# Attention and gated mixing on one Trainium2 core: another hand-written order of the second part's stages

## The chip, the cores and the metric

The kernel runs on one core of a Trainium2 chip. The metric is the device time of one execution in microseconds (us). The kernel before takes 1852.48 us (median of 3 runs, 1850.31 to 1857.23).

## What is computed

For 8 batches of 2048 tokens with 256 features: layer norm, Nystrom attention with 16 heads and 64 landmarks, an output product, layer norm, residual; then layer norm, a gated mixing block with a shift by one token, layer norm, residual. Cut to what matters:

```
k, q, v = heads(norm(x) @ Wk), heads(norm(x) @ Wq) / 4, heads(norm(x) @ Wv)
q_l, k_l = means of q and k over groups of 32 tokens         # 64 landmarks
s1 = softmax(q @ k_l.T)      s2 = softmax(q_l @ k_l.T)      s3 = softmax(q_l @ k.T)
z = pinv(s2)                                                # 6 iterations
x = x + norm((s1 @ (z @ (s3 @ v))) @ Wo + bo)
h = norm(x);  d = shift(h) - h
r = sigmoid(xr @ W_r.T),  k = relu(xk @ W_k.T) ** 2          # xr, xk: h mixed with shift(h) by mu_r, mu_k
x = x + norm(r * (k @ W_v.T))
```

## The kernel before

Part one computes the landmarks and the inverses of all batches. It is the same in both kernels and ends at about 415 us. Part two goes through the batches; each batch is cut into four tiles (0 to 3) of 512 tokens. A stage is a short piece of work on a tile, and its name stands for what every engine does for it:

- XA normalizes the input (VectorE, `xhat`), R transposes it (TensorE) and splits it into a high and a low half (ScalarE and VectorE, `xT`). AQ, AK and AV are the projections to queries, keys and values. KC copies the keys by 12 DMAs into `k_stack`.
- B1 and B2 multiply keys with the landmarks' queries, and VectorE takes row maxima (L1257). C1 and C2 multiply queries with the landmarks' keys, and VectorE takes token maxima (L1265). M spreads the row maxima into `q_stack`, which stage S loads by 24 DMAs.
- FS (0 to 7) scores keys against landmarks, ScalarE takes the exponential (L915), FV multiplies it with the values and VectorE adds to `uT`. W and V apply the inverse.
- D, E1 and E2 are the token scores of a tile: D transposes the maxima, E1 and E2 multiply, ScalarE takes the exponential (L938). H applies them. O is the output product; VectorE then adds the bias and takes the statistics of a norm.
- OA applies this norm (VectorE), and GpSimd adds the residual (`xm`, L737). N takes statistics of the sum, NA applies them (`x2h`), T transposes (ScalarE copies to `x2T`, GpSimd subtracts, `xkT`, L747), TA mixes (VectorE, `xrT` and `xkT`, L1338).
- GR is the gate's product (L1777, ScalarE L971 and GB), GK the keys' (L1787), G2 the last (L1799, VectorE multiplies with the gate into `ob`). GS takes statistics, GA applies them, and GpSimd adds the residual (L753). GO writes the tile; XR loads the residual.

TensorE writes to three pairs of PSUM tensors, `bank`, `wide` and `acc`, shared by all stages: B, C, FS and E use `wide`. A stage may write to a pair when the reader of its last use has drained it.

The order of part two is written out by hand. `PRO` lists (stage, tile) for the start; `BODY` lists (stage, tile, offset of the batch) for one turn and is run seven times; `LAST` is the last turn. `part2_program` walks the joined list on each engine and issues that engine's share of each stage, so all five engines work in the same order, and waits are on semaphores that count uses:

```
        order = [(name, c, 0) for name, c in PRO]
        order += [(name, c, b + d) for b in range(B - 1) for name, c, d in BODY if b + d >= 0]
        order += [(name, c, B - 1 + d) for name, c, d in LAST]
```

A stage with offset -1 belongs to the batch before: the second half of a batch (its gates above all) runs between the projections of the next. Such a stage is written below as GR(1) for tile 1.

Of the kernel before, what the change touches and what calls it, by code (L numbers as in the profile page):

```python
# [15 lines left out]
def sandwich(nc, x, Wk, Wq, Wv, Wo, bo, W_r, W_k, W_v, mu_r, mu_k, out):  # L16
# [10 lines left out]
    H, HS, M, ITERS = 16, 16, 64, 6  # L27
# [12 lines left out]
    with ctx:  # L40
# [55 lines left out]
        GR = 4  # L96
# [19 lines left out]
        X = [sb(f"X{s}", [P, PAIRS, M], c=part1) for s in ROWS]  # L116
# [199 lines left out]
        class Norm:  # L316
# [40 lines left out]
            def apply(self, dve, dst, src, g, c):  # L357
# [58 lines left out]
        PRO = [("R", 0), ("X", 2), ("X", 3), ("Q", 0), ("AK", 0), ("XA", 2),  # L416
# [3 lines left out]
        BODY = [("C1", 2, 0), ("R", 3, 0), ("GK", 1, -1), ("C2", 2, 0), ("O", 3, -1), ("B2", 2, 0), ("T", 2, -1),  # L420
# [53 lines left out]
        counted, used = (0, 0, 0), {}  # L474
# [1357 lines left out]
```

## Time and profile before

| | |
|---|---|
| median of 3 runs | 1852.48 us (1850.31 to 1857.23) |
| the profiled execution's own time | 1859.59 us |
| its span, first to last instruction | 1857.9 us |
| granted TensorE clock, mean | 0.945 |
| busy: TensorE / VectorE / ScalarE / GpSimd | 1575.4 / 1370.3 / 1041.2 / 278.4 us |
| first FS of the first batch | 492.17 us |
| from then, per batch | 164.6, then five times 170.8 |
| the last batch's first FS | 1685.59 us |

The trace gives the start of each instruction in us from the span's start, its duration, and in brackets how long its engine had sat idle before it and what released it. Instructions of a kind in a row are merged; x4 is their count, and the duration is that of all together.

### The profile page before, as it was taken

What the parts mean: (1) busy time and instruction counts of PE and PEld (TensorE: products, weight loads), DVE (VectorE), ACT (ScalarE), POOL (GpSimd) and SP (SyncE); (2) the same over time, 40 slices, a digit from 0 to 9 for tenths busy, and PEclk for the clock granted to TensorE, in tenths of its full rate; (3) what the DMA queues carried; (4) which work ended last, traced back from release to release, by engine and by line L of the source; (5) the groups of instructions that cost most, each with busy time, mean ns of one, the idle gap of its engine ahead of it and who ended that gap; (6) DMA issues with size and microseconds to landing.
All of it is one profiled execution on the core that took longest, in us unless ns stands there. A gap on an engine that the chain in (4) does not pass through costs nothing. (4 is left out here: it accounts for less than half of the span.)

```text
span 1857.9 us, 50685 instructions
## 1 busy us (share of the span) xinstructions
PE 1575.4 (85%) x21132; PEld 1087.1 (59%) x21132; DVE 1370.3 (74%) x3068; ACT 1041.2 (56%) x1663; POOL 278.4 (15%) x163
## 2 busy tenths in 40 slices
PE   4778888787689889899889998998989899988885
PEld 2768767773455564465456555644655565546453
DVE  6887777777558966895797579668947975795475
ACT  1689769972354465455545554654455455535452
POOL 5200020000001111121111111111211121110122
PEclk9789989998899999999999999999999999999898
DMA  8300100002211312131322122221213211221111
GB/s 272 97 5 4 60 22 29 3 26 67 72 41 42 73 54 56 50 80 34 92 54 58 50 58 69 58 55 50 73 41 92 54 51 55 61 58 33 36 35 35
DMA packets 125844, 104.66 MB, mean 56 GB/s; under 512 B 30513, under 2 KB 123569, under 8 KB 125617
## 3 DMA queue, kind: packets, MB, share of 16 engines
q1 hardware_dynamic: 125616, 101.42, 19.5%
q8 instruction: 169, 2.77, 0.6%
q14 instruction: 59, 0.48, 0.1%
HBM read 56.23 MB, written 19.92 MB: 41 GB/s over the span
## 5 line engine op out<-in xcount | busy, mean ns | idle before, releaser
L938 ACT ACTIVATE p<-wide 128x1024 f32<-128x1024 f32 x128 | 124.0, 1021 | 123.0 <-PE wide L1717 122.3
L1265 DVE TENSOR_REDUCE m<-wide 128x16 f16<-128x1024 f32 x128 | 150.6, 1218 | 39.9 <-PE wide L1601 39.6
L1777 PE MATMUL bank<-wrT,xrT 128*128 128x256 f32 x512 | 139.5, 433 | 43.8 <-ACT vv L904 35.9
L915 ACT ACTIVATE e<-wide 128x1024 f32<-128x1024 f32 x128 | 124.5, 1021 | 79.6 <-PE wide L1634 68.3
L1257 DVE TENSOR_REDUCE m<-wide 128x2 f32<-128x1024 f32 x128 | 150.0, 1215 | 2.9 <-PE wide L1581 2.9
L1777 PEld LDWEIGHTS bank<-wrT,xrT 128*128 128x128 f32 x512 | 109.4, 219 | 68.9 <-issue 39.8
L753 POOL TENSOR_TENSOR ob<-ob,xm 128x1024 f32<-128x1024 f32 x32 | 77.0, 2406 | 480.6 <-DVE ob L361 480.6
L1757 PE MATMUL bank<-wo,oT 128*128 128x256 f32 x512 | 120.9, 390 | 6.2 <-DVE xT L1225 3.6
L747 POOL TENSOR_TENSOR xkT<-x2T 128x1024 f32<-128x1024 f32 x32 | 60.7, 1897 | 430.5 <-ACT x2T L963 430.5
L1787 PE MATMUL acc<-xkT,wkT 128*128 128x512 f32 x256 | 118.8, 608 | 7.1 <-DVE xkT L1338 7.1
L737 POOL TENSOR_TENSOR xm<-yy,xres 128x1024 f32<-128x1024 f32 x32 | 78.2, 2443 | 307.0 <-DVE yy L361 163.9
L1799 PE MATMUL bank<-wvT,ka 128*128 128x256 f32 x512 | 119.3, 387 | 0.8 <-ACT x2T L963 0.4
L1757 PEld LDWEIGHTS bank<-wo,oT 128*128 128x128 f32 x512 | 96.4, 193 | 25.7 <-issue 8.3
L1799 PEld LDWEIGHTS bank<-wvT,ka 128*128 128x128 f32 x512 | 96.5, 192 | 16.2 <-issue 2.3
L1301 DVE TENSOR_TENSOR oT<-acc,oT 128x512 f32<-128x512 f32 x64 | 42.2, 682 | 81.3 <-ACT oT L949 81.1
L1653 PE MATMUL acc<-e,vv 128*17 128x64 f32 x4096 | 76.4, 222 | 25.5 <-ACT e L915 21.7
L971 ACT ACTIVATE sg<-bank 128x512 f32<-128x512 f32 x64 | 38.1, 597 | 104.4 <-PE bank L1777 84.9
L1543 PE MATMUL acc<-xT,w 128*128 128x512 f16 x384 | 92.1, 391 | 1.7 <-DVE xT L1225 1.7
L1543 PE MATMUL bank<-xT,w 128*128 128x512 f16 x384 | 89.4, 383 | 3.8 <-ACT x2T L963 1.9
L1565 PE MATMUL bank<-w,xT 128*128 128x256 f16 x768 | 89.2, 273 | 4.0 <-ACT x2T L963 2.8
L1653 PEld LDWEIGHTS acc<-e,vv 128*17 128x17 f32 x4096 | 61.1, 98 | 43.0 <-issue 25.8
L1565 PEld LDWEIGHTS bank<-w,xT 128*128 128x128 f16 x768 | 72.9, 98 | 21.0 <-issue 5.3
(284 smaller groups left out, 3796.9 us busy)
## 6 DMA issues: line engine op xcount, KB each, us to landing
x1in<-in_L_attn_x SPq DMA_DIRECT2D x8, 2048.0 KB, 8.3
xin<-in_L_attn_x SPq DMA_DIRECT2D x32, 512.0 KB, 4.2
k_stack<-kh SPq DMA_DIRECT2D x256, 64.0 KB, 2.0
xres<-in_L_attn_x SPq DMA_DIRECT2D x32, 512.0 KB, 4.1
out<-ob SPq DMA_DIRECT2D x32, 512.0 KB, 5.1
k_stack<-kl SPq DMA_DIRECT2D x128, 64.0 KB, 2.0
q_stack<-landmarks SPq DMA_DIRECT2D x192, 4.0 KB, 1.6
inverse<-X SPq DMA_DIRECT2D x8, 256.0 KB, 2.0
```

The source lines that it names most:

```text
L737: g.tensor_tensor(xm[c % 3][:, :, :], yy[:, :, :], xres[:, :, :], ALU.add).then_inc(xm_made, 1)
L915: sc.activation(e3[w][:, :], wide[w][:, :], ACT.Exp).then_inc(wide_drained[w], 1)
L938: sc.activation(p1[:, 2 * j:2 * j + 2, :], wide[w][:, :].rearrange("p (a n) -> p a n", a=2), ACT.Exp).then_inc(wide_drained[w], 1)
L1257: v.tensor_reduce(m3[:, 2 * j:2 * j + 2, c], wide[j % 2][:, :].rearrange("p (a n) -> p a n", a=2), AX.X, ALU.max).then_inc(wide_drained[j ...
L1265: v.tensor_reduce(m1[:, tiles, 2 * w:2 * w + 2, :].rearrange("p t q x -> p q t x"), wide[w][:, :].rearrange("p (q t x m) -> p q t x m", q= ...
L1543: ins = mm(dst[o][:, :], w16[:, w, wt, k, o * P:(o + 1) * P], xT[:, xt, k, :], start=(i == 0), stop=(i == len(TERMS) - 1))
L1565: ins = mm(bank[j][:, t * A:(t + 1) * A], xT[:, xt, k, tok], w16[:, 2, wt, k, :], start=(i == 0), stop=(i == len(TERMS) - 1))
L1653: ins = mm(acc[k][32 * q:32 * q + HS + 1, j * M:(j + 1) * M], vv[:, 2 * i + w, h, :], e3[w][:, h * M:(h + 1) * M], start=(w == 0 and j == ...
L1757: ins = mm(dst, oT[:, k, tok], wo[:, k, :], start=(k == 0), stop=(k == KB - 1))
L1777: ins = mm(bank[j][:, t * A:(t + 1) * A], xrT[:, k, tok], wrT[:, k, :], start=(k == 0), stop=(k == KB - 1))
L1787: ins = mm(acc[o][:, :], wkT[:, k, o * P:(o + 1) * P], xkT[:, k, :], start=(k == 0), stop=(k == KB - 1))
L1799: ins = mm(bank[j][:, t * A:(t + 1) * A], ka[:, k, tok], wvT[:, k, :], start=(k == 0), stop=(k == KB - 1))
```

## The change

The three lists `PRO`, `BODY` and `LAST` are replaced. The stages are the same 1108, each once for its tile and batch, and no stage's code is touched; only their order differs. Where the turn begins moves as well: `PRO` has 11 entries where it had 30, and `BODY` starts earlier in the batch, which by itself changes nothing. A few lines of the table:

```diff
-        PRO = [("R", 0), ("X", 2), ("X", 3), ("Q", 0), ("AK", 0), ("XA", 2),
...
+        PRO = [("R", 0), ("K", 0), ("AQ", 0), ("X", 2), ("XA", 2),
+               ("AK", 0), ("C1", 0), ("AV", 0), ("Q", 0), ("R", 1), ("B1", 0)]
...
-                ("B1", 3, 0), ("OA", 3, -1), ("GS", 1, -1), ("KC", 3, 0), ("AV", 3, 0), ("B2", 3, 0), ("GR", 2, -1),
...
+                ("G2", 1, -1), ("TA", 2, -1), ("D", 0, 0), ("GS", 1, -1), ("AK", 3, 0), ("GR", 2, -1), ("GB", 2, -1),
+                ("GO", 0, -1), ("B1", 3, 0), ("AV", 3, 0), ("B2", 3, 0), ("GK", 2, -1), ("M", 0, 0), ("OA", 3, -1),
```

GR(2) and its GB stand in front of AV of tile 3, where they stood behind it; D, E1, E2 and H of the last tile have offset -1. All line numbers below `BODY` are larger by 5 in the changed kernel.

Three places of the order. The first is VectorE in a steady turn. Before, from the multiplication of G2(0) (`ob`) to the row maxima of tile 2; L361 on `yy` is OA(2), `xhat` is XA of tile 3, `xrT` and `xkT` are TA(1):

```order
L1355 TENSOR_TENSOR ob<-bank,sg 128x512 x2
L361 TENSOR_SCALAR yy<-yy,norm_y_mv,norm_y_rstd 128x256 x4
L1207 TENSOR_SCALAR xhat<-xin,mv,rstd 128x256 x4
L335 BN_STATS norm_f_st<-ob 128x6 x4
L343 BN_AGGR norm_f_mv<-norm_f_st 128x2 x4
L1338 SCALAR_TENSOR_TENSOR xrT<-xkT,mu,x2T 128x512 x2
L1338 SCALAR_TENSOR_TENSOR xkT<-xkT,mu,x2T 128x512 x2
L1344 COPY x2T<-x2T 128x2
L335 BN_STATS norm_m_st<-xm 128x6 x4
L343 BN_AGGR norm_m_mv<-norm_m_st 128x2 x4
L1301 TENSOR_TENSOR oT<-acc,oT 128x512 x2
L1257 TENSOR_REDUCE m<-wide 128x2 x2
```

After, from the output product of O(2) to the token maxima of tile 1; L361 on `yy` is OA(2) again:

```order
L1314 TENSOR_TENSOR yy<-bank,bo_all 128x512 x2
L335 BN_STATS norm_y_st<-yy 128x6 x4
L343 BN_AGGR norm_y_mv<-norm_y_st 128x2 x4
L1230 TENSOR_TENSOR xT<-bank,xT 128x512 x2
L361 TENSOR_SCALAR yy<-yy,norm_y_mv,norm_y_rstd 128x256 x4
L1343 SCALAR_TENSOR_TENSOR xrT<-xkT,mu,x2T 128x512 x2
L1343 SCALAR_TENSOR_TENSOR xkT<-xkT,mu,x2T 128x512 x2
L1349 COPY x2T<-x2T 128x2
L335 BN_STATS norm_f_st<-ob 128x6 x4
L343 BN_AGGR norm_f_mv<-norm_f_st 128x2 x4
L1306 TENSOR_TENSOR oT<-acc,oT 128x512 x2
L1270 TENSOR_REDUCE m<-wide 128x2x2x4 x2
```

XA of tile 3 no longer stands between OA(2) and TA(1); TA(1) follows OA(2) at once, and the statistics of N(2) (L335, L343 on `norm_m_st`) have moved behind H and the maxima.

The second is TensorE in the first batch, from R of tile 2 on (L1536 before, L1541 after is R; L1581/L1586 B; L1601/L1606 C; L1543/L1548 AQ on `bank` and AK on `acc`; L1565/L1570 AV). Before:

```order
L1536 MATMUL bank<-ident,xhat 128x128 x8
L1601 MATMUL wide<-kA_bd,qh 128x128 x16
L1543 MATMUL bank<-xT,w 128x512 x12
L1601 MATMUL wide<-kA_bd,qh 128x128 x16
L1581 MATMUL wide<-kh,q_bd 128x512 x4
L1543 MATMUL acc<-xT,w 128x512 x12
L1601 MATMUL wide<-kA_bd,qh 128x128 x16
L1565 MATMUL bank<-w,xT 128x256 x24
L1601 MATMUL wide<-kA_bd,qh 128x128 x16
L1581 MATMUL wide<-kh,q_bd 128x512 x4
L1601 MATMUL wide<-kA_bd,qh 128x128 x16
L1536 MATMUL bank<-ident,xhat 128x128 x8
```

After:

```order
L1541 MATMUL bank<-ident,xhat 128x128 x8
L1606 MATMUL wide<-kA_bd,qh 128x128 x16
L1548 MATMUL bank<-xT,w 128x512 x12
L1586 MATMUL wide<-kh,q_bd 128x512 x4
L1548 MATMUL acc<-xT,w 128x512 x12
L1570 MATMUL bank<-w,xT 128x256 x24
L1606 MATMUL wide<-kA_bd,qh 128x128 x16
L1541 MATMUL bank<-ident,xhat 128x128 x8
```

In both excerpts the last row is R of tile 3. Before, seven products of B and C stand between R(2) and R(3), some of them next to each other; after, three do, and each has a projection or a transpose on at least one side.

The third is TensorE in `LAST`, from M of the last batch. L1634/L1639 is FS, L1653/L1658 FV, L1799/L1804 G2, L1787/L1792 GK, L1777/L1782 GR. Before:

```order
L1616 MATMUL bank<-ident,m3m 32x128 x8
L1601 MATMUL wide<-kA_bd,qh 128x128 x16
L1693 MATMUL bank<-ident,m 4x128 x16
L1634 MATMUL wide<-q_stack,k_stack 128x128 x16
L1799 MATMUL bank<-wvT,ka 128x256 x8
L1714 MATMUL wide<-m1T,neg_sel 128x512 x4
L1717 MATMUL wide<-qh,kE_bd 128x512 x4
L1717 MATMUL wide<-ql,kE_bd 128x512 x4
L1717 MATMUL wide<-qh,kE_bd 128x512 x4
L1653 MATMUL acc<-e,vv 17x64 x32
L1634 MATMUL wide<-q_stack,k_stack 128x128 x16
L1653 MATMUL acc<-e,vv 17x64 x32
```

After:

```order
L1621 MATMUL bank<-ident,m3m 32x128 x8
L1570 MATMUL bank<-w,xT 128x256 x24
L1639 MATMUL wide<-q_stack,k_stack 128x128 x16
L1792 MATMUL acc<-xkT,wkT 128x512 x4
L1639 MATMUL wide<-q_stack,k_stack 128x128 x16
L1658 MATMUL acc<-e,vv 17x64 x32
L1782 MATMUL bank<-wrT,xrT 128x256 x8
L1658 MATMUL acc<-e,vv 17x64 x32
L1639 MATMUL wide<-q_stack,k_stack 128x128 x16
L1804 MATMUL bank<-wvT,ka 128x256 x8
L1606 MATMUL wide<-kA_bd,qh 128x128 x16
L1658 MATMUL acc<-e,vv 17x64 x32
```

AV of tile 3, GK(2) and GR(2) of batch 6 now stand behind M; they stood in front of it. GK(3) and G2(3) of batch 6, in the loop before, come after W now.

## Rows read from the trace of the kernel before

**Rows 1.** The page, part 1: busy time, share of the span and instructions of each engine.

```profile
PE 1575.4 (85%) x21132; PEld 1087.1 (59%) x21132; DVE 1370.3 (74%) x3068; ACT 1041.2 (56%) x1663; POOL 278.4 (15%) x163
```

**Rows 2.** Busy time by stretch; columns: from:to, length, busy us per engine, PEclk, DMA share, GB/s.

```profile
415.00:492.00 77.00, 52.40 (x384) 28.36 (x384) 56.61 (x75) 18.80 (x32) 3.06 (x6) 0.84 0.30 73
...
827.40:998.20 170.80, 154.07 (x1653) 97.62 (x1652) 129.36 (x283) 90.98 (x150) 26.59 (x12) 0.97 0.22 60
...
1510.60:1685.60 175.00, 154.99 (x1657) 97.57 (x1655) 131.34 (x286) 91.05 (x151) 28.48 (x13) 0.95 0.21 57
1685.60:1858.00 172.40, 132.06 (x1306) 87.54 (x1306) 93.83 (x248) 80.13 (x131) 36.67 (x15) 0.90 0.10 32
```

**Rows 3.** TensorE in order of time, a steady turn: E1, E2 of tile 3, GR(1), GR(2).

```profile
753.16 0.40 PE L1714 MATMUL wide<-m1T,neg_sel 4*128 4x512 f16 x4 [1.59 <-DVE m L1265]
...
773.17 0.39 PE L1714 MATMUL wide<-m1T,neg_sel 4*128 4x512 f16 x4
...
778.09 0.40 PE L1581 MATMUL wide<-kh,q_bd 32*128 32x512 f16 x4
778.42 2.79 PE L1565 MATMUL bank<-w,xT 128*128 128x256 f16 x24
786.33 5.38 PE L1777 MATMUL bank<-wrT,xrT 128*128 128x256 f32 x16 [5.12 <-ACT vv L904]
...
814.58 3.72 PE L1777 MATMUL bank<-wrT,xrT 128*128 128x256 f32 x16
```

**Rows 4.** ScalarE, the same place: the root of N(2)'s norm.

```profile
785.26 0.20 ACT L351 ACTIVATE norm_m_ln<-norm_m_mv 128x4 f32<-128x4 f32 x1 [4.23 <-DVE norm_m_mv L343]
```

**Rows 5.** VectorE, the same place.

```profile
775.16 3.44 DVE L1207 TENSOR_SCALAR xhat<-xin,mv,rstd 128x256 f32<-128x256 f32 x4
778.52 1.39 DVE L335 BATCH_NORM_STATS2 norm_f_st<-ob 128x6 f32<-128x256 f32 x4
...
780.39 1.38 DVE L1338 SCALAR_TENSOR_TENSOR xrT<-xkT,mu,x2T 128x512 f32<-128x512 f32 x2
781.69 1.41 DVE L1338 SCALAR_TENSOR_TENSOR xkT<-xkT,mu,x2T 128x512 f32<-128x512 f32 x2
...
785.08 1.26 DVE L1301 TENSOR_TENSOR oT<-acc,oT 128x512 f32<-128x512 f32 x2
786.26 2.35 DVE L1257 TENSOR_REDUCE m<-wide 128x2 f32<-128x1024 f32 x2
```

**Rows 6.** GpSimd, the same place.

```profile
775.39 2.42 POOL L737 TENSOR_TENSOR xm<-yy,xres 128x1024 f32<-128x1024 f32 x1 [3.44 <-issue]
```

**Rows 7.** VectorE in the last turn: TA(1).

```profile
1792.11 3.48 DVE L1338 SCALAR_TENSOR_TENSOR xrT<-xkT,mu,x2T 128x512 f32<-128x512 f32 x2
```

**Rows 8.** GpSimd in the last turn, beside it.

```profile
1789.18 1.90 POOL L747 TENSOR_TENSOR xkT<-x2T 128x1024 f32<-128x1024 f32 x1
1792.27 2.78 POOL L753 TENSOR_TENSOR ob<-ob,xm 128x1024 f32<-128x1024 f32 x1 [1.20 <-DVE ob L361]
```

**Rows 9.** TensorE, steady turn of batch 3: C2 of tile 0 and GR(0).

```profile
1089.10 0.41 PE L1601 MATMUL wide<-kA_bd,qh 32*128 32x128 f16 x16 [1.37 <-DVE m L1257]
1089.44 5.41 PE L1777 MATMUL bank<-wrT,xrT 128*128 128x256 f32 x16
```

**Rows 10.** TensorE's waits from 415 to 488 us; columns: us in total, times, longest.

```profile
PE wide L1581 <- DVE m L1265: 7.5, 6, 2.3
```

**Rows 11.** The DMA queue of SyncE in the first batch.

```profile
449.56 11.31 SPq L562 DMA_DIRECT2D q_stack<-landmarks  x24
...
481.53 5.06 SPq L613 DMA_DIRECT2D k_stack<-kh  x8
486.64 2.51 SPq L613 DMA_DIRECT2D k_stack<-kl  x4
```

**Rows 12.** TensorE's waits from 1685.6 to 1727 us, the last batch's FS and FV.

```profile
PE acc L1653 <- ACT e L915: 5.4, 10, 1.2
```

**Rows 13.** TensorE in the last turn: GR(1).

```profile
1795.65 6.03 PE L1777 MATMUL bank<-wrT,xrT 128*128 128x256 f32 x16 [4.62 <-DVE xrT L1338]
```

More of the change, by code:

```diff
@@ L408, in sandwich @@
         fin_out = [sem(f"fin_out{i}") for i in range(2)]
-        PRO = [("R", 0), ("X", 2), ("X", 3), ("Q", 0), ("AK", 0), ("XA", 2),
[3 rows of a table removed]
-        BODY = [("C1", 2, 0), ("R", 3, 0), ("GK", 1, -1), ("C2", 2, 0), ("O", 3, -1), ("B2", 2, 0), ("T", 2, -1),
[19 rows of a table removed]
-        LAST = [("C1", 2, 0), ("R", 3, 0), ("GK", 1, -1), ("C2", 2, 0), ("GO", 0, -1), ("O", 3, -1), ("KC", 2, 0),
[18 rows of a table removed]
+        PRO = [("R", 0), ("K", 0), ("AQ", 0), ("X", 2), ("XA", 2),
+               ("AK", 0), ("C1", 0), ("AV", 0), ("Q", 0), ("R", 1), ("B1", 0)]
+        BODY = [("AQ", 1, 0), ("KC", 0, 0), ("B2", 0, 0), ("XR", 1, -1), ("AK", 1, 0), ("X", 3, 0), ("T", 0, -1),
[19 rows of a table added]
+        LAST = [("KC", 0, 0), ("AQ", 1, 0), ("X", 3, 0), ("XA", 3, 0), ("B2", 0, 0), ("XR", 1, -1), ("AK", 1, 0),
[25 rows of a table added]
         USES = {"R": (1, 0, 0), "AQ": (1, 0, 0), "AK": (0, 0, 1), "AV": (1, 0, 0), "B1": (0, 1, 0), "B2": (0, 1, 0),
```

81 rows, old and new, of tables (BODY, LAST, PRO) are left out of this document.

## The prediction

> **What bounds the kernel now.** First the busy shares [rows 1]: TensorE is busy for 85% of the span and VectorE for 74%, so no engine is full, and an order can lose or gain only waiting time. Then the stretches [rows 2]: part two starts with a stretch of 77 us in which VectorE is the busier engine (56.6 us against 52.4), goes through steady turns of 170.8 us in which TensorE is busy for 154.1 us and VectorE for 129.4 us, and ends with 175.0 us (from the last but one batch's first FS to the last batch's) and 172.4 us, in which TensorE is busy for only 132.1 us. A steady turn therefore holds 16.7 us without TensorE, the rest after the last FS 40.3 us.
>
> Then TensorE in order of time, to find the largest wait. In each steady turn it is in front of GR(1), 5.12 us [rows 3]. The row names ScalarE's copy of the values, but this copy stands on ScalarE behind the root of N(2)'s norm, which waited 4.23 us for VectorE [rows 4]. VectorE is the late one: it works without a pause through XA (3.44 us), GS(0), TA(1) and N(2) [rows 5]. XA is long because GpSimd's `xm` of OA(2) runs beside it [rows 6]; four instructions of this form take 1.4 us otherwise, so 2.0 us are a hold. After the wait GR(1) takes 5.38 us where GR(2) takes 3.72 [rows 3]: TensorE was at the lower of its two clock levels (1.2 instead of 2.4 GHz), which costs 1.66 us more. So this place costs 6.8 us in a turn.
>
> **The change, part by part.** No instruction is added or removed. The work of each engine stays, and what is priced is waiting, place by place, by the order and the durations of the rows.
>
> The old place. In the new order XA is away from OA(2), and AV's copy stands far from N(2)'s root: the 5.12 us and the slow product there go. Gain 6.8 us in a turn.
>
> The new GR(1). TA(1) now follows OA(2) at once on VectorE, and GpSimd starts `xm` when OA(2) ends. The rows of the last turn show this pair: `xrT` beside a GpSimd instruction takes 3.48 us instead of 1.38 [rows 7, 8], a hold of 2.1 us. GR(1) waits for `xrT`. From T(1) on, the chain is its copy (about 1 us), R's copy, the root, OA(2) with 1.4, then 3.5: about 8.5 us. TensorE has R, E2, H and C2 in front of GR(1); E2 and H take 4.9 us [rows 3], all of it about 7. Wait: 1.5 us.
>
> Behind it, B1 of tile 2 needs the pair `wide`, which C2 of tile 1 leaves when VectorE has reduced it. VectorE has, after `xrT`, still `xkT` 1.4, GS(0) 1.9 with its second instruction, H 1.3 and the reduction 2.35 [rows 5], 6.9 us; TensorE has only GR(1), 3.7 us. Wait: 3.2 us. Queued behind B1 are AQ of tile 3 and GK(1), which wait for nothing themselves.
>
> GK(0) waits for TA(0) and for VectorE's share of H. VectorE has OA(1) (1.4, held for some 0.9 by `xkT` on GpSimd, 1.90 us long [rows 8]), a reduction 2.35, N(1) 1.9, TA(0) 2.8 and H 1.3, 10.7 us; TensorE has D, C, AV 2.8 [rows 3], H (4.9 less about 1 of E2), B and R, about 8.4 us. Wait: 2.3 us.
>
> O(1) stands closer behind O(0), since AK and AV of tile 0 were moved ahead, and waits for R's share on VectorE: 1.3 us. D of tile 0 stands behind G2(1) and waits until VectorE, held by `xkT` in GA(0), has multiplied G2(1): 1.2 us. These five come to 9.5 us. In the old turn the corresponding ones are 5.12, 1.66 of slow clock, 1.37 in front of C2 [rows 9] and 1.59 in front of E1 of tile 3 [rows 3], 9.7 us. Among the eight FS, three have no other work between them and their FV where two and a half had; that is about half a microsecond against the change. Taken together a steady turn stays where it is: 0, with ends of -3 (the slow clock does not come back and a third of the waits overlap) and +4 (it comes back twice, and the holds of OA(1), TA(1), GA(0) and TA(2) add up to 6 us where two holds gave 4). For the six turns from the first batch's FS to the seventh's: 0, ends -18 and +24.
>
> The start. Before the first M the old order has clumps of B and C, each of which waits for VectorE to reduce the product before: 7.5 us in six waits for B alone [rows 10]. The new one alternates them with projections [the second order excerpt] and has one C less in front of M (2.35 us). Then the copies into `k_stack` decide: S's 24 take 11.3 us in the queue, KC(2) stands behind them, and ScalarE can't overwrite the keys of tile 3 before KC(2) has landed, at about 470.5 by the same rows moved; KC(3) follows from about 472 on and takes 7.6 us [rows 11], and FS comes some 3 us after, as now (489.2 and 492.2): the first FS at 482 instead of 492. Gain 10 us; ends 4 (if the copies, not VectorE, set most of the start already) and 14 (the 7.5 us, the C, and the waits of C and M beside them).
>
> The end. Of the last turn GK(2) and GR(2), up to 3.7 us each, T(3) with about 1 and two C of 0.4 [rows 9] move behind the last batch's first FS: about 9 us less in the stretch of 175.0 us, taken as 8. They land in the loop of FS and FV, where TensorE waits 5.4 us for exponentials in ten places [rows 12]; with GK(3) and G2(3) leaving the loop it has as much work as before in fewer waits: 3 us less. GK(3) and G2(3), some 7.2 us, now lie behind W, where the chain through the tiles and not TensorE's work sets the time; half of them is taken as hidden, +3.6. In exchange GA(0) no longer stands in front of TA(1) there, whose wait of 4.62 us and slow product (6.03 for 3.72) go [rows 13]: -6.9, so the tail gives 3. The end: -14, ends -22 and -4 (the moved products delay W and the chain as a whole).
>
> Sum: -10 + 0 - 14 = -24 us on the profiled execution's own 1859.59 us (its span of 1857.9 and 1.7 around it): 1835.6. That execution was 7.1 us above the median of 1852.48, so the forecast is 1852.5 - 24 = 1828.5, rounded to 1829.
>
> **Two rules of the skill.** `xrT` beside a GpSimd instruction takes 3.48 us against 1.38, a hold until that instruction has ended [rows 7, 8]. The Trainium skill (GPSIMD Engine Reference, Specifications) says that the two share their SBUF interfaces and contend when VectorE has two SBUF inputs or a two-port mode; it gives no size. If contention only slowed VectorE to half, `xrT` beside GpSimd would take 2.8 instead of 3.5 and the new GR(1) wait would be 0.8; the measured row decides.
>
> The granted clock fell also behind a wait of only 1.37 us: GR(0) took 5.41 us in the turn of batch 3 [rows 9]. The Trainium skill (TensorE: Matmul & The Clock Gate, HAM oscillation) ties the fall to idle gaps of TensorE. It stands beside the rival that follows.
>
> **The rivals.** *Full clock.* If only the long wait lowers the clock, its removal keeps every steady turn at 2.4 GHz: 1.66 us in six turns, -10, so 1819. For it: each turn of the old kernel falls right behind the 5.12 us. Against it: the 5.41 us row. Chance 0.10.
>
> *The backlog goes altogether.* VectorE has 41 us to spare in a turn; if the spread is even enough, none of the five new waits comes, and six turns give 6.8 us each: -41 - 24, 1787. Against it: two holds now sit in front of products. Chance 0.12.
>
> *The edges give nothing.* The first FS is bound by the chain of copies at 490, and the moved products lengthen the tail as much as they leave the turn; with a turn 0.5 us better, 1848. For it: the queue rows. Chance 0.21.
>
> *Slower: TA(1) and TA(2) are held.* Both mixes start beside a GpSimd instruction, each 2.1 us late; GR(1), B1, GK(1) and O(3) queue behind, and the waits of 1.5 and 3.2 us, close together, lower the clock for GR(1) and again for AQ: +6 in a turn, +36 - 24 = +12, 1864. It decides from +4 us in a turn (174.8) on, where it eats the edges. For it: `xrT` at 3.48 us. Against it: the old order has two holds in a turn too. Chance 0.13.
>
> **How the numbers follow.** The forecast as summed has 0.44; its own range, from the ends of the edges and a third of those of the turns, is 1806 to 1846. About 0.5% (9.3 us) is what a measurement of this kernel can tell from no change. Faster takes the forecast, the full clock and the vanished backlog, 0.66; within it the vanished edges, 0.21; slower 0.13. The range reaches from -50 (full ends of start and end with a turn 2.3 us shorter) to +4: 1802 to 1857. It leaves out the vanished backlog and the slower case.
>
> **What the new profile would show.** Right: the first FS at 482 and the seventh 1018 us later, as now (164.6 + 5 x 170.8); no wait over 4 us in a steady turn; `xrT` of TA(1) at 3.5 us each turn; waits in front of B1 of tile 2 for the maxima (L1265, now L1270) near 3 us; the last batch's first FS about 167 us after the seventh's. Wrong, if the steady turn is off 170.8 by more than 3 us, if the first FS comes after 488, or if the stretch behind the last FS is longer than 173 us.

## The result and the profile after

The changed kernel takes 1846.4 us in the median of 12 runs (1841.5 to 1850.4), the kernel before 1858.3 in the same comparison: ratio 0.9933, 95% interval 0.9913 to 0.9952, that is 12 us less (9 to 16). The direction was right; of the 24 us forecast half came. The forecast of 1829 us started from 1852.5; in this comparison the kernel before stands at 1858.3. The measured 1846.4 lies 0.4 us above the forecast's own range (1806 to 1846) and inside the wide one (1802 to 1857). One execution of the run "turn and tail" below was far slower (6520.1 us) and stands outside its ratio; the median of the other four is 1816.3.

The profiled execution took 1844.38 us (before 1859.59), 15.2 less. 5.2 of these lie in part one, whose code is the same: part two's first transposition is at 411.67 us instead of 416.92, and in the runs below it lies anywhere from 411 to 420. So stretches are compared from there on.

Windows of the changed kernel, columns as in [rows 2]: the first projection to the first FS(0), the first turn, a steady one, from the seventh batch's FS(0) to the last batch's, and the rest, whole and cut at W.

```profile
415.07:479.63 64.56, 49.83 (x376) 26.71 (x377) 49.37 (x61) 18.30 (x32) 0.02 (x1) 0.88 0.36 85
479.63:648.75 169.12, 148.70 (x1602) 93.48 (x1603) 115.95 (x235) 84.61 (x135) 17.07 (x8) 0.93 0.20 51
990.24:1160.84 170.60, 153.16 (x1651) 96.51 (x1650) 130.82 (x284) 91.86 (x150) 26.81 (x13) 0.98 0.23 60
1502.05:1665.30 163.25, 144.13 (x1595) 90.03 (x1594) 120.11 (x268) 85.44 (x138) 24.81 (x12) 0.96 0.22 58
1665.30:1842.70 177.40, 139.91 (x1372) 93.09 (x1369) 102.73 (x278) 87.08 (x143) 38.60 (x17) 0.91 0.10 34
...
1665.30:1705.95 40.65, 35.78 (x755) 28.01 (x752) 23.60 (x70) 26.22 (x38) 8.98 (x4) 0.96 0.09 28
1705.95:1842.70 136.75, 104.13 (x618) 65.08 (x618) 79.13 (x209) 60.86 (x106) 29.62 (x13) 0.89 0.11 35
```

| stretch | before | after | difference | forecast |
|---|---|---|---|---|
| first transposition to first FS(0) | 75.3 | 68.0 | -7.3 | -10 |
| first turn | 164.9 | 169.1 | +4.2 | 0 |
| five steady turns | 853.3 | 853.3 | 0 | 0 |
| seventh FS(0) to eighth | 175.3 | 163.3 | -12.0 | -8 |
| loop of FS and FV | 41.2 | 40.7 | -0.5 | -3 |
| behind W | 131.1 | 136.8 | +5.6 | -3 |
| sum | | | -10.0 | -24 |

(The loop and the part behind W were 41.20 and 131.11 us in the windows of before, cut at 1726.79. Read from the first instruction of one FS(0) to that of the next, the first turn before is 164.9 us and the steady ones 170.4 to 170.9.)

Steady turns were forecast as unchanged in sum, with one large wait replaced by five small ones. The groups by line show it over the whole run (busy, mean ns of one | idle before). Kernel before, the gate's product, the keys', the projection to queries, B:

```profile
L1777 PE MATMUL bank<-wrT,xrT 128*128 128x256 f32 x512 | 139.5, 433 | 43.8 <-ACT vv L904 35.9 <-DVE xrT L1338 7.9
L1787 PE MATMUL acc<-xkT,wkT 128*128 128x512 f32 x256 | 118.8, 608 | 7.1 <-DVE xkT L1338 7.1
L1543 PE MATMUL bank<-xT,w 128*128 128x512 f16 x384 | 89.4, 383 | 3.8 <-ACT x2T L963 1.9 <-DVE xT L1225 1.9
L1581 PE MATMUL wide<-kh,q_bd 32*128 32x512 f16 x256 | 27.8, 392 | 9.1 <-DVE m L1265 7.5 <-issue 1.5
```

The same groups of the changed kernel:

```profile
L1782 PE MATMUL bank<-wrT,xrT 128*128 128x256 f32 x512 | 119.9, 388 | 8.7 <-DVE xrT L1343 8.7
L1792 PE MATMUL acc<-xkT,wkT 128*128 128x512 f32 x256 | 127.3, 643 | 31.2 <-DVE oT L1306 24.6 <-DVE xkT L1343 6.6
L1548 PE MATMUL bank<-xT,w 128*128 128x512 f16 x384 | 107.9, 440 | 3.3 <-DVE xT L1230 3.3
L1586 PE MATMUL wide<-kh,q_bd 32*128 32x512 f16 x256 | 30.2, 399 | 24.3 <-DVE m L1270 18.7 <-DVE kl L1243 5.6
```

The gate's product lost 19.6 us of busy time (slow clock) and 35.1 of waiting, 54.7 in all. Some 47 of them are the 6.8 us of [rows 3] in seven turns; four slow GR(0) like that of [rows 9] add 6.8. Against this, the keys' product took 32.6 us more, the query projection 18.0 (all of it slow clock), B 17.6.

One steady turn of the changed kernel, TensorE (batch 3), from H on; then VectorE and GpSimd at the same place:

```profile
1080.95 3.67 PE L1792 MATMUL acc<-xkT,wkT 128*128 128x512 f32 x8 [2.78 <-DVE oT L1306]
...
1114.28 3.72 PE L1782 MATMUL bank<-wrT,xrT 128*128 128x256 f32 x16 [0.87 <-DVE xrT L1343]
1120.10 0.54 PE L1586 MATMUL wide<-kh,q_bd 32*128 32x512 f16 x2 [2.10 <-DVE m L1270]
1121.14 0.60 PE L1586 MATMUL wide<-kh,q_bd 32*128 32x512 f16 x2 [0.50 <-DVE m L1270]
1121.68 5.30 PE L1548 MATMUL bank<-xT,w 128*128 128x512 f16 x12
```
```profile
1110.71 3.51 DVE L1343 SCALAR_TENSOR_TENSOR xrT<-xkT,mu,x2T 128x512 f32<-128x512 f32 x2
...
1110.93 2.75 POOL L742 TENSOR_TENSOR xm<-yy,xres 128x1024 f32<-128x1024 f32 x1 [1.43 <-issue]
```

`xrT` stands for 2.1 us beside `xm`; B1(2) is late by what VectorE lost there, and AQ(3) behind it runs at the lower clock (5.30 us; other projections take 2.76). Behind W there are two such places. At OA(0) the old order had no hold. TA(0) follows OA(1) in both orders, but the pair came out the other way round. Before, `xm` was the one held (4.72 us; 2.35 is usual), `xrT` and `xkT` ran freely, and VectorE stood only at the small copy behind them (2.20 us for 0.17):

```profile
1766.81 1.41 DVE L1338 SCALAR_TENSOR_TENSOR xrT<-xkT,mu,x2T 128x512 f32<-128x512 f32 x2
...
1769.58 2.20 DVE L1344 COPY x2T<-x2T 128x2 f32<-128x2 f32 x1
...
1767.03 4.72 POOL L737 TENSOR_TENSOR xm<-yy,xres 128x1024 f32<-128x1024 f32 x1 [2.14 <-DVE yy L361]
```

After, `xrT` itself stood (second row below), and GK(0) waited 4.50 us:

```profile
1731.31 3.40 DVE L361 TENSOR_SCALAR yy<-yy,norm_y_mv,norm_y_rstd 128x256 f32<-128x256 f32 x4
...
1731.47 2.45 POOL L758 TENSOR_TENSOR ob<-ob,xm 128x1024 f32<-128x1024 f32 x1 [29.32 <-DVE ob L361]
...
1748.43 3.50 DVE L1343 SCALAR_TENSOR_TENSOR xrT<-xkT,mu,x2T 128x512 f32<-128x512 f32 x2
...
1736.01 6.37 PE L1762 MATMUL bank<-wo,oT 128*128 128x256 f32 x16 [1.46 <-DVE oT L1306]
...
1754.21 5.80 PE L1792 MATMUL acc<-xkT,wkT 128*128 128x512 f32 x8 [4.50 <-DVE oT L1306]
...
1781.27 5.41 PE L1782 MATMUL bank<-wrT,xrT 128*128 128x256 f32 x16 [3.36 <-DVE xrT L1343]
```

In sum the holds behind W did not grow. Against the median of its own kind, VectorE's instructions there took 9.0 us more before and 7.6 after. What differs is where they stand.

### The profile page after: what moved, and what is told of

It is laid out like the page before. It is cut to its first block and busy times, and to the rows that moved or that the text cites. A ratio compares the mean times of both kernels' runs of the same rounds, so it can differ in the third digit from the quotient of the medians.

```text
span 1842.7 us, 50685 instructions
## 1 busy us (share of the span) xinstructions
PE 1561.4 (85%) x21132; PEld 1074.1 (58%) x21132; DVE 1370.4 (74%) x3068; ACT 1046.8 (57%) x1663; POOL 276.7 (15%) x163
## 3 DMA queue, kind: packets, MB, share of 16 engines
q1 hardware_dynamic: 125616, 101.42, 19.6%
## 5 line engine op out<-in xcount | busy, mean ns | idle before, releaser
L1792 PE MATMUL acc<-xkT,wkT 128*128 128x512 f32 x256 | 127.3, 643 | 31.2 <-DVE oT L1306 24.6
L1782 PE MATMUL bank<-wrT,xrT 128*128 128x256 f32 x512 | 119.9, 388 | 8.7 <-DVE xrT L1343 8.7
L1804 PE MATMUL bank<-wvT,ka 128*128 128x256 f32 x512 | 117.7, 383 | 0.4 <-ACT x2T L968 0.4
L1782 PEld LDWEIGHTS bank<-wrT,xrT 128*128 128x128 f32 x512 | 97.3, 194 | 26.4 <-DVE xrT L1343 10.6
L1548 PE MATMUL bank<-xT,w 128*128 128x512 f16 x384 | 107.9, 440 | 3.3 <-DVE xT L1230 3.3
L1792 PEld LDWEIGHTS acc<-xkT,wkT 128*128 128x128 f32 x256 | 51.6, 210 | 89.7 <-issue 55.0
L1804 PEld LDWEIGHTS bank<-wvT,ka 128*128 128x128 f32 x512 | 94.9, 190 | 14.2 <-issue 1.5
L986 ACT ACTIVATE ka<-acc 128x512 f32<-128x512 f32 x64 | 38.2, 597 | 112.1 <-PE acc L1792 112.1
L1658 PE MATMUL acc<-e,vv 128*17 128x64 f32 x4096 | 76.0, 224 | 25.5 <-ACT e L920 15.3
L1548 PE MATMUL acc<-xT,w 128*128 128x512 f16 x384 | 91.0, 388 | 0.0
L1570 PE MATMUL bank<-w,xT 128*128 128x256 f16 x768 | 89.3, 273 | 0.1
L1639 PE MATMUL wide<-q_stack,k_stack 97*128 97x128 f16 x1024 | 75.5, 226 | 12.4 <-DVE m L1270 12.3
L1658 PEld LDWEIGHTS acc<-e,vv 128*17 128x17 f32 x4096 | 62.1, 99 | 39.9 <-issue 17.4
```

The costliest lines, as they stand in the source:

```text
L1548: ins = mm(dst[o][:, :], w16[:, w, wt, k, o * P:(o + 1) * P], xT[:, xt, k, :], start=(i == 0), stop=(i == len(TERMS) - 1))
L1570: ins = mm(bank[j][:, t * A:(t + 1) * A], xT[:, xt, k, tok], w16[:, 2, wt, k, :], start=(i == 0), stop=(i == len(TERMS) - 1))
L1658: ins = mm(acc[k][32 * q:32 * q + HS + 1, j * M:(j + 1) * M], vv[:, 2 * i + w, h, :], e3[w][:, h * M:(h + 1) * M], start=(w == 0 and j == ...
L1782: ins = mm(bank[j][:, t * A:(t + 1) * A], xrT[:, k, tok], wrT[:, k, :], start=(k == 0), stop=(k == KB - 1))
L1792: ins = mm(acc[o][:, :], wkT[:, k, o * P:(o + 1) * P], xkT[:, k, :], start=(k == 0), stop=(k == KB - 1))
L1804: ins = mm(bank[j][:, t * A:(t + 1) * A], ka[:, k, tok], wvT[:, k, :], start=(k == 0), stop=(k == KB - 1))
```

## The experiments

The theory after this reading: **VectorE's time lost to holds by GpSimd, and the slow clock behind the waits, are the price**; the rivals were VectorE's sum of work whatever the holds, work put off past a mark, and the tail's longer chain. The edits move entries of the tables; `move(table, stage, where, other)` does that to one. Ratios are to the kernel before, each with its interval. Summary:

| run | edit on | median us | ratio |
|---|---|---|---|
| changed kernel | | 1846.4 | 0.9933 (0.9913 to 0.9952) |
| start only | before | 1853.1 | 0.9998 (0.9962 to 1.0033) |
| end only | before | 1845.7 | 0.9958 (0.9924 to 0.9993) |
| XA later | before | 1843.9 | 0.9944 (0.9917 to 0.9971) |
| C1 ahead of FS(0) | changed | 1847.6 | 0.9929 (0.9902 to 0.9956) |
| TA(1) first | changed | 1827.0 | 0.9845 (0.9801 to 0.9888) |
| GS(0) between | changed | 1830.6 | 0.9850 (0.9815 to 0.9884) |
| tail, two moves | changed | 1846.1 | 0.9933 (0.9911 to 0.9955) |
| tail, four places | changed | 1838.5 | 0.9914 (0.9885 to 0.9944) |
| GK(3) in the loop | changed | 1855.3 | 0.9987 (0.9965 to 1.0009) |
| turn, three moves | changed | 1823.3 | 0.9821 (0.9788 to 0.9854) |
| turn and tail | changed | 1816.8 | 0.9782 (0.9749 to 0.9816) |
| turn and tail, mended | changed | 1788.3 | 0.9627 (0.9590 to 0.9663) |

### Start and end alone

```diff
+        order = joined(PRO, BODY, LAST)
+        order = order[:order.index(("FS", 0, 0))]
+        order += [key for key in joined(PRO2, BODY2, LAST2) if key not in order]
```

Here the first lists are those of the change and the second those of before; in the run of the end it is the other way round, cut at FS(0) of the seventh batch.

> The changed kernel's order up to the first batch's FS(0), from there on the order of before. The profile of the changed kernel showed 64.6 us from the first projection to that FS(0) instead of 72.5, and then a first turn of 169.2 us instead of 164.6. Theory (the start is a gain of its own; the longer first turn is the new turn's doing): 64.6 again, then a first turn of 164 to 166 and steady turns of 170.8: 7 to 8 us less than before, ratio 0.996. Rival (what the start gains, the loop behind it gives back, because the copies, the values or VectorE's backlog set its pace): 64.6, then a first turn of 168 to 170, in all 3 to 4 us less, ratio 0.998.

FS(0) came 72.2 us behind the first transposition, not 68.0, and the first turn took 164.7. The two together, 236.9 us, are what the changed kernel has (237.1; before 240.1). So 3 us up to the second FS(0) are a gain. The mark itself moved by 4 us less, because the old order, put behind the cut, brought C1 of tile 3 in front of it. Neither expectation held as written: the start was longer than both had it, and the first turn is the theory's. What the place of C1 is worth is asked below. The ratio, with an interval of 7 parts in a thousand, can't tell 3 us.

> The order of before up to the seventh batch's FS(0), from there on the changed order. Theory (stretch and tail belong to the new order alone): from the seventh's FS(0) to the last's 163 to 165 us (175.0 before), from there to the end 177 to 178 (172.4 before), in all 5 to 7 us less, ratio 0.9965. Rival (the long tail is what the new turns hand down, such as work left over): the stretch at 165 and the tail at 172 to 173, in all 10 us less, ratio 0.9945. All six turns before it stay at 164.6 and five times 170.8 in both.

```profile
1500.73:1658.77 158.04, 139.59 (x1578) 88.21 (x1579) 115.45 (x254) 85.48 (x137) 24.03 (x11) 0.99 0.23 60
1658.77:1835.80 177.03, 139.30 (x1372) 90.94 (x1369) 102.68 (x278) 86.98 (x143) 38.61 (x17) 0.93 0.11 34
```

The windows from the seventh and the eighth FS(0). The tail is long here too, behind old turns: it belongs to the new `LAST`. The stretch is 5 us shorter than I expected. By the lists it holds less: the old order has C1, N and NA of tile 3 in front of this FS(0), the new one behind it, and VectorE works 4.7 us less in it than in the changed kernel (115.45 for 120.11). The five turns before, in the order of the kernel before, scattered from 167.4 to 170.5 us. In all five the wait in front of E1 of tile 3 was absent and GR(0) slow; GR(1) took 6.46 and 6.68 us in the two long ones (169.5 and 170.5) and 5.08 to 5.23 in the others.

### The start's mark

```diff
+        order.remove(("C1", 3, 0))
+        order.insert(order.index(("FS", 0, 0)), ("C1", 3, 0))
```

> The changed kernel with one stage of one batch moved: C1 of tile 3 of the first batch in front of FS(0). It asks whether the earlier FS(0) is a gain or work put off. From part two's first transposition to FS(0) it was 68.0 us in the changed kernel (75.3 before), to the second FS(0) 237.1 (240.1 before). Theory (of the 7.3 us, about 4 are C1 and what goes with it, which the first turn then pays): FS(0) 2 to 4 us later, the first turn 2 to 4 us shorter than 169.1 (or than the 167.4 to 168.3 of the runs with the same first turn), 236 to 238 together, and the whole within 2 us of the changed kernel. Rival (the loop has room for it): FS(0) later and the first turn the same, in all 2 to 4 us more.

FS(0) came 3.9 us later (71.9), the first turn took 166.9, in sum 238.7 us (0.7 over the theory's 238), and the whole time was unchanged. The first turn of the changed kernel's order was 167.4, 168.3 and twice 169.1 us in its traces, so it gave 0.5 to 2.2 of the 3.9 us back: work put off is little more than half of it at most. Still, one stage of 0.4 us on TensorE and 2.35 on VectorE moves the mark by 4 us and leaves the whole as it was: an earlier FS(0) is no gain by itself. Nor do the copies set the new mark. In the changed kernel the last copy into `k_stack` was issued at 475.2 us and landed 2.9 us later, 1.6 us ahead of FS(0) at 479.63, which waited for VectorE's maxima; before, the last one (issued at 488.55, 3.3 us) had landed only 0.3 us ahead.

The turn of batch 3 in this trace tells what the slow clock costs there. Its waits are those of the other turns (0.87 us in front of GR(1), 2.10 and 0.65 in front of B1(2)), but AQ(3) was fast, and the turn took 168.0 us where the four others took 170.6 to 171.0:

```profile
1126.25 2.76 PE L1550 MATMUL bank<-xT,w 128*128 128x512 f16 x12
```

### The old place

```diff
+        move(BODY, ('XA', 3, 1), 'behind', ('N', 2, 0))
```

> The kernel before with one stage moved in BODY: XA of tile 3 behind N(2), so that its xhat does not run beside GpSimd's xm and does not stand ahead of N(2)'s root. It asks what the old 5.12 us in front of GR(1) and the slow product were worth, which I priced at 6.8 us in a turn. Theory (hold and place of XA make the wait): xhat takes 1.4 us instead of 3.44, the wait is 1.7 us or less, GR(1) takes 3.7 us instead of 5.38 unless a short wait is enough for the fall of the clock: a turn of 164 to 167.5, 24 to 45 us less than before. Rival (R(3) at the next place waits for xhat, or VectorE's backlog makes the wait elsewhere): a turn of 169 to 171, at most 12 us less.

```profile
946.77 5.38 PE L1783 MATMUL bank<-wrT,xrT 128*128 128x256 f32 x16 [2.33 <-ACT vv L910]
...
1080.21 5.41 PE L1783 MATMUL bank<-wrT,xrT 128*128 128x256 f32 x16
```

`xhat` took 1.35 us and the wait fell from 5.1 to 2.3 in every turn. GR(1) was still slow in three of the five steady turns (first row) and at full clock, 3.69 us, in two; in these two C of tile 2 waits 2.2 us for VectorE. GR(0) is slow in three (second row). The turns were 165.9 to 170.0 us, 168.0 in the mean: 2.7 less, between the two expectations. So the hold and the place of XA made 2.8 of the 5.1 us of wait, and nearly all of that came. What the other 2.3 us and the slow product would bring no run shows.

### The new place, in two ways

```diff
+        move(BODY, ('TA', 1, -1), 'in front of', ('OA', 2, -1))
```

> The changed kernel with TA(1) in front of OA(2) in BODY, so that GpSimd's xm no longer starts beside xrT. Theory (GpSimd holds VectorE, the products behind it wait and the clock falls): xrT goes from 3.51 to 1.4 us, GR(1) waits for nothing (0.87 now), B1(2) waits about 0.5 to 1 us (2.6 now) and AQ(3) takes 2.8 us instead of 5.3: a steady turn of 165.5 to 168 instead of 170.7, and over seven turns 19 to 35 us less than the changed kernel: 1811 to 1827. Rival (VectorE is late in this place by its sum of work, and the hold only moves waiting about): xrT at 1.4, but OA(2), N(2) and O(3) later by what TA(1) now takes ahead of them; the waits come back at AQ(3), GK(1) or O(3), a turn of 170 to 171.5 and the time of the changed kernel within 5 us.

TensorE, VectorE and GpSimd of the turn of batch 3:

```profile
1106.65 3.72 PE L1788 MATMUL bank<-wrT,xrT 128*128 128x256 f32 x16
...
1111.40 0.39 PE L1592 MATMUL wide<-kh,q_bd 32*128 32x512 f16 x2 [1.02 <-DVE m L1276]
1112.44 0.39 PE L1592 MATMUL wide<-kh,q_bd 32*128 32x512 f16 x2 [0.65 <-DVE m L1276]
1112.76 2.76 PE L1554 MATMUL bank<-xT,w 128*128 128x512 f16 x12
...
1102.85 1.42 DVE L1349 SCALAR_TENSOR_TENSOR xrT<-xkT,mu,x2T 128x512 f32<-128x512 f32 x2
...
1107.21 2.36 POOL L748 TENSOR_TENSOR xm<-yy,xres 128x1024 f32<-128x1024 f32 x1 [4.40 <-issue]
```

A swap of two neighbours takes 16 us off the changed kernel's ratio of 0.9933. In this turn the waits and AQ(3) are the theory's, number by number; B1(2) waits 1.67 us instead of 2.6. The slow clock did not leave the turn, though: here GK(0) took 5.37 us where it had taken 3.67, and in the first two steady turns, where GK(0) was fast, AQ(3) took 4.45. The five steady turns are 167.3 to 167.6 us either way. The move also put `xrT` earlier by the order alone, which the next one excludes:

```diff
+        move(BODY, ('GS', 0, -1), 'in front of', ('TA', 1, -1))
```

> The changed kernel with one stage moved in BODY: GS(0), statistics that were not held beside GpSimd so far, between OA(2) and TA(1). TA(1) then still follows OA(2) and xrT is ready no earlier than now (OA(2) ends at 1110.8 in the turn of batch 3, 1.9 us of statistics, 1.4 and a rest of the hold: about 1114.3 against 1114.2), but VectorE works through xm's 2.4 us instead of standing. Theory (a hold costs VectorE's time, which everything behind it pays): GR(1) waits 0.9 to 1.4 us as now, B1(2) 0.5 to 1.2 instead of 2.6, AQ(3) takes 2.8 instead of 5.3: a turn of 167 to 169. Rival (only the date of xrT counts, which the first experiment also moved 1.4 us forward by the order alone): a turn of 170 to 171.5.

```profile
1109.94 1.40 DVE L335 BATCH_NORM_STATS2 norm_f_st<-ob 128x6 f32<-128x256 f32 x4
1111.81 1.94 DVE L1349 SCALAR_TENSOR_TENSOR xrT<-xkT,mu,x2T 128x512 f32<-128x512 f32 x2
...
1110.16 2.38 POOL L748 TENSOR_TENSOR xm<-yy,xres 128x1024 f32<-128x1024 f32 x1 [1.43 <-issue]
...
1113.80 3.72 PE L1788 MATMUL bank<-wrT,xrT 128*128 128x256 f32 x16 [1.16 <-DVE xrT L1349]
1118.80 0.39 PE L1592 MATMUL wide<-kh,q_bd 32*128 32x512 f16 x2 [0.65 <-DVE m L1276]
1119.12 2.76 PE L1554 MATMUL bank<-xT,w 128*128 128x512 f16 x12
```

`xrT` is no earlier and GR(1) waits even longer (1.16), but VectorE did its statistics under `xm` at their full 1.40 us. B1's waits fall to 0.9 (0.23 and 0.65), AQ(3) is fast, the turns are 167.5 to 169.3; GK(0), whose wait of 2.8 us is unchanged, is slow in every turn (5.07 to 6.66 us). A rest of the hold, 0.5 us, is left. What VectorE lost to the hold was the price, not the date of `xrT`.

### The tail

```diff
+        move(LAST, ('OA', 0, 0), 'behind', ('H', 1, 0))
+        move(LAST, ('TA', 0, 0), 'in front of', ('OA', 1, 0))
```

> The changed kernel with two moves in LAST: OA(0) behind H(1) and TA(0) in front of OA(1), so that neither yy nor xrT starts beside a GpSimd instruction. The stretch behind the last W took 136.8 us instead of 131.2. Theory (the two new holds and the slow products behind them made the tail longer): yy 1.4 us instead of 3.40, xrT 1.4 instead of 3.50, O(1) and GK(0) start 1.3 us earlier each and at least one of them is not slow (6.37 and 5.80 us now, 3.7 at full clock): the stretch at 129 to 133, 4 to 8 us less than the changed kernel. Rival (the tail is longer because GK(3) and G2(3) of the batch before now stand in it): at most 2 us less.

```profile
1706.51:1839.70 133.19, 102.75 (x618) 63.99 (x618) 75.12 (x209) 60.74 (x106) 29.12 (x13) 0.92 0.11 36
```

Behind W 133.2 us, 3.6 less than 136.8, just outside the 4 to 8 expected and far more than the GK(3) rival's 2. It rests on one execution, but a steady number: in six traces with the changed `LAST` the stretch from the last FS(0) to the end is 177.1 to 177.4 us, and here it is 173.9. `yy` took 1.37 us and `xrT` 1.42; O(1) (5.22 us) and GK(0) (5.37, its wait 1.8 us instead of 4.5) still ran slowly. The runs don't show the gain (the ratio is that of the changed kernel); 3.6 us are less than half the width of its interval.

```diff
+        move(LAST, ('GA', 1, 0), 'behind', ('TA', 3, 0))
+        move(LAST, ('T', 1, 0), 'in front of', ('OA', 2, 0))
+        move(LAST, ('GS', 0, 0), 'in front of', ('OA', 2, 0))
+        move(LAST, ('TA', 1, 0), 'in front of', ('OA', 2, 0))
```

> The same, and two more places in LAST, which were alike before the change: GA(1) behind TA(3), and T(1), GS(0), TA(1) in front of OA(2). Theory (holds): GR(1) waits for nothing instead of 3.36 us, GK(3) waits about 2 instead of 4.62, and both take 3.7 us instead of 5.41 and 5.87: 6 to 10 us less than with the first two moves alone. Rival (the chain through a tile sets the tail, so that OA(2), now later, delays O(3), T(2) or GK(2) by as much): within 2 us of the first two moves.

```profile
1713.69:1842.00 128.31, 100.70 (x618) 62.53 (x618) 71.73 (x209) 60.41 (x106) 28.71 (x13) 0.93 0.12 38
...
1789.35 5.37 PE L1803 MATMUL acc<-xkT,wkT 128*128 128x512 f32 x8 [3.58 <-DVE oT L1317]
```

4.9 us less again, under the 6 to 10 expected: GR(1) and GK(3) are fast (3.72 and 3.70 us), but GK(1) now waits 3.6 us for H(3)'s share, which stands on VectorE behind N(2), and that for `xm`. From the last FS(0) it is 169.0 us. VectorE's busy time behind W fell from 79.1 to 71.7 us without one instruction less: 7.4 us of holds. The ratios of the two tail runs and of the changed kernel overlap in their intervals, so the tail's gain is read from these stretches.

```diff
+        move(LAST, ('GK', 3, -1), 'behind', ('GR', 3, -1))
+        move(LAST, ('GB', 3, -1), 'behind', ('GK', 3, -1))
+        move(LAST, ('G2', 3, -1), 'behind', ('FV', 7, 0))
+        move(LAST, ('GS', 3, -1), 'behind', ('G2', 3, -1))
```

> The changed kernel with GK(3), GB(3), G2(3) and GS(3) of the seventh batch moved back in LAST from behind W into the end of the loop of FS and FV, where they stood before the change. The prediction took half of their 7.2 us as hidden behind W and the loop as 3 us shorter without them; the changed kernel showed the loop only 0.6 us shorter and the stretch behind W 5.6 longer. Theory (both products keep TensorE busy in a stretch where it has idle time between the tiles' chains, so that moved back they cost the loop about 6 us and give the tail at most 3 to 4): 2 to 4 us more than the changed kernel. Rival (they lengthen the tail by all of their 7.2 us and the loop has waits to take them): 2 to 5 us less.

```profile
1665.77:1714.18 48.41, 42.97 (x780) 32.64 (x777) 25.21 (x73) 31.14 (x43) 8.97 (x4) 0.96 0.07 24
1714.18:1850.40 136.22, 98.56 (x593) 58.19 (x593) 77.22 (x206) 55.81 (x100) 29.67 (x13) 0.89 0.11 35
```

From the last FS(0) to the end it is 184.6 us, 7.2 more. In these windows, cut at the second of W's two transpositions, which waits here, the loop grew by 7.8 us and the part behind W shrank by 0.5; cut at the first, at 1713.14, they are 6.7 and 0.5 more. Either way both products were hidden within 0.5 us where the change had put them, and the rival is out. It cost 10 us in the ratio, more than the 2 to 4 expected.

### A version that beats both

```diff
+        move(BODY, ('TA', 1, -1), 'in front of', ('OA', 2, -1))
+        move(BODY, ('GA', 0, -1), 'in front of', ('B2', 2, 0))
+        move(BODY, ('N', 1, -1), 'behind', ('GR', 0, -1))
```

> The changed kernel with TA(1) in front of OA(2) in BODY as before, and two more moves there: GA(0) in front of B2(2), so that VectorE is not held beside xkT of T(2) and xrT of TA(2) not beside ob; and N(1) behind GR(0), so that TA(0) and the values' H stand 1.9 us earlier. With the first move alone a turn took 167.5 us. Theory (what is left in a turn is GK(0)'s 2.8 us, D(0)'s 1.3 us and the holds): these two waits go to about 0.9 and 0, a turn of 163.5 to 166, in all 10 to 25 us less than with the first move alone. Rival (VectorE's backlog only moves on: D(0)'s wait becomes one for O(3), N(1)'s root comes late for NA(1) and T(1)): a turn of 167 to 168.

```profile
1286.38 1.38 DVE L361 TENSOR_SCALAR ob<-ob,norm_f_mv,norm_f_rstd 128x256 f32<-128x256 f32 x4 [2.93 <-ACT norm_f_rstd L354]
...
1290.77 1.94 PE L1779 MATMUL bank<-ident,x2h 128*128 128x128 f32 x8 [2.56 <-DVE yy L1322]
```

GK(0)'s wait fell from 2.8 to 0.8 us, but the turns stayed at 167.2 in the mean, as the rival had it, for a cause that neither named: GA(0) stood behind GK(1) on ScalarE too, its root came late, VectorE waited 2.93 us for it, and T(2) and a slow G2(1) paid. The waits are the same in all five steady turns, yet these took 164.8 to 169.2 us, and the slow products follow the difference: none in the turn of 164.8, AQ(3) with 1.7 us in that of 166.5, the same and G2(1) with 2.2 in that of 169.2.

With the six tail entries added:

> All seven moves together. If the places are independent, the sum of what they give apart: the steady turn of the run with three moves in BODY and the tail of the run with four in LAST, 10 us less than the former, 1797 to 1815 us. Rival (a shorter turn hands VectorE's work down to the tail): the tail gives back half of it.

The turns stayed at 167.3 us and the tail fell to 168.7 (177.2 in the run before): the places add up, though at 1816.8 us the time missed the 1797 to 1815 expected. Then the two waits seen were mended:

```diff
-        move(BODY, ('GA', 0, -1), 'in front of', ('B2', 2, 0))
+        move(BODY, ('GA', 0, -1), 'in front of', ('GK', 1, -1))
+        move(LAST, ('N', 2, 0), 'behind', ('H', 3, 0))
```

> The version with moves in BODY and LAST, mended where its trace showed two waits: GA(0) stands in front of GK(1) and not behind it, since its root came 2.9 us late from ScalarE and T(2) then waited 2.6 us for O(3)'s sum; and in LAST N(2) stands behind H(3), since VectorE waited 2.5 us for xm with H(3)'s share queued behind, and GK(1) waited 3.6 us. Theory: T(2)'s wait at 0.3 to 0.5 again, G2(1) not slow (5.85 us in most turns), a turn of 163.5 to 166; the tail 3 to 5 us shorter than 168.7: 1790 to 1805. Rival (what each move frees, the next stage waits for): within 5 us of the version it mends.

```profile
969.18:1133.05 163.87, 151.59 (x1651) 96.00 (x1650) 126.60 (x284) 91.71 (x150) 26.43 (x13) 0.99 0.23 62
1621.53:1786.00 164.47, 134.00 (x1372) 87.45 (x1369) 95.44 (x278) 86.64 (x143) 37.69 (x17) 0.95 0.11 36
```

Steady turns of 162.7 (AQ(3) fast) to 163.9 us (AQ(3) at 4.45), a tail of 164.5, both as expected, the sum a little better: 1788.3 us, 69 us (3.7%) under the kernel before and 57 under the changed one by the ratios. VectorE is busy for 126.6 us in a turn instead of 130.8; the 4.2 are holds.

## Why the prediction was right and wrong

**The steady turn: right, in part by luck.** Forecast 0, measured 0. Its five waits were each within 0.65 us: GR(1) 0.87 (1.5), B1(2) 2.6 in two (3.2), O(1) 1.17 (1.3), D(0) 1.25 in two (1.2), and GK(0) 2.78 (2.3), 8.7 in all against 9.5. No wait was over 4 us and `xrT` took 3.51. The slow clock stayed and changed its place, from GR(1) to AQ(3), where it costs 2.5 us that the sum of 9.5 does not hold; I had it only as part of the slower rival. On the other side the 9.7 us of the old turn leave out the slow GR(0) that [rows 9] shows. The row groups confirm the 6.8 us of the old place as measured where it stood. That their removal gives nothing in sum was forecast and came; how much of them could be had, no run shows whole.

**The start: -10 was mis-taken.** Measured -7.3 to the mark and -3.1 up to the next one. Two steps failed. "Then the copies into `k_stack` decide": they had landed 1.6 us before FS(0), which waited for VectorE's maxima, and one C ahead of it made it 3.9 us later. And the first turn, counted among the six at 0, took 4.2 us more: I priced C1 of tile 3 leaving the start as a gain and not as a cost behind it. With C1 ahead the first turn is 166.9, so up to 2.2 of the 4.2 us are that stage. The other 2.0 belong to the waits of the new order's first turn: with TA(1) first it is 164.9 again. No run separates the two further. The 7.5 us of waits for B shrank to 3.9; of the clumps themselves, no run was made.

**The end: -14 was half wrong.** The stretch gave more than its term (-12.0 for -8): the new lists also put OA(3), N(3) and NA(3) of batch 6 behind the last FS(0), and TensorE's busy time in it fell by 10.9 us, VectorE's by 11.2 ([rows 2] against the window above). The tail's term is the step that failed most, -3 against +5.6 behind W and -0.5 in the loop:
- "GK(3) and G2(3), half hidden, +3.6": they are hidden whole (without them the part behind W stays within 0.5 us).
- "GR(1)'s wait and slow product go, -6.9": GA(0) went, but xrT stood behind `xm` and N(2) instead; the wait was 3.36 and the product 5.41, together 1.9 us less than [rows 13].
- What was not in the sum at all: OA(0) now beside `ob` of GA(3), and `xrT` of TA(0) now held by `xm` of OA(1), where before it was the other way round. Their removal takes 3.6 us off.
- I had listed the hold of TA(1) in the turn and not asked the same of `LAST`, which is another list. With 1.9 us gained at GR(1), the tail lost some 7.5 elsewhere; beyond these 3.6 near 4 us have no run of their own, and their cause stays open.

**The loop's 3 us** did not come: its waits for exponentials fell from 5.4 to 1.7 us in [rows 12]'s terms, but GK(2), GR(2), C2 of tile 2 and C1 of tile 3 filled it (TensorE busy 35.8 us for 34.8).

**The rivals.** *Full clock* fell: the keys' and query products took the slow clock over. *The backlog goes altogether* fell as the place for the change as made, though a neighbouring order reaches 163.8 us. *The edges give nothing* was half true. *Slower*: both holds came (2.1 and 1.2 us), the clock fell for AQ(3), not for GR(1); it did not reach +4, since the old turn had paid as much.

**The range.** The ends as listed (edges -36 and -8, a third of the turns' -18 and +24) come to 1810 to 1852, not to the 1806 to 1846 written; 1846.4 lies inside the former. Of the three signs of being wrong one came: the stretch behind the last FS was 177.4 us, above 173.

## What to carry to other kernels

Look for pairs that start together, an instruction of GpSimd and one of VectorE like `xrT` (two inputs from SBUF) or `yy` and `xhat` (one, with per-token scalars); each costs VectorE up to about GpSimd's whole duration (2.1 us beside 2.75 here), and one entry moved between them gives most of it back: statistics (1.40 us) and reductions from PSUM (1.21 us each) took no longer beside GpSimd in any trace read. Check each written-out list for it apart, the last turn too. When a milestone comes earlier, ask what work it no longer has in front, and judge by the next milestone. A wait's length is what it costs where it stands; what its removal brings is what the next late engine leaves of it. Here the 6.8 us in front of GR(1) went, and the steady turn stayed as it was.

## What the hardware showed that was not expected

Holds last until the GpSimd instruction ends and are not half speed: `xrT` beside `xm` took 3.51 us, where half speed would give 2.8, and ended 0.5 us behind `xm`; the statistics beside the same `xm` took 1.40, as always. The Trainium skill (SBUF — State Buffer, SBUF: two separate sides) says that the port pair shared by the two engines is an exclusive lock: a VectorE instruction in a two-port mode, or with two SBUF inputs against a GpSimd one that reads SBUF, and the GpSimd instruction exclude each other, the first to start has the pair to its end, and the other blocks. By that rule the trace agrees, and the prediction's price for half speed was not needed. `yy`, of one tensor and per-token scalars, is held too (3.40 us beside `ob`).

Who is held can change from one execution to the next. In the traces of the two tail runs the steady turn has the changed kernel's order, and `xm` starts 0.2 us behind `xrT` as there. But in 11 of their 12 places `xm` was the one held and took 4.7 us (2.75 there); `xrT` took 1.4, and VectorE lost 2.0 us at the small copy behind `xkT`. The steady turns were no shorter for it (170.6 to 172.4 us): VectorE paid in either case.

The same waits do not give the same clock. In front of AQ(3) stood 1.02 and 0.65 us in the run with TA(1) first and in the mended version; it took 2.76 us in the rows shown of the one and 4.45 in these of the other:

```profile
1094.94 0.39 PE L1601 MATMUL wide<-kh,q_bd 32*128 32x512 f16 x2 [1.02 <-DVE m L1285]
1095.98 0.39 PE L1601 MATMUL wide<-kh,q_bd 32*128 32x512 f16 x2 [0.65 <-DVE m L1285]
1096.31 4.45 PE L1563 MATMUL bank<-xT,w 128*128 128x512 f16 x12
```

That is the mended version, which waits least. Within the former trace both durations occur too. Turns in one and the same order took 167.4 to 170.5 us within one execution. So a term for the slow clock is good to a few us in a turn at best, and what decides each fall stays open.
